# Hybrid attention and mixture block on one core: later input loads, numerators swapped in their own buffer, second weights taken by quarters, and new instruction orders

## The reference, cut to what matters

```python
x = x + attn_a(layernorm(x), w_qkv, w_o)
x = x + ffn(layernorm(x), gate_w, base_w, base_b, lora_A, lora_B)
x = x + attn_b(layernorm(x), wq, wk, wv, wo)
x = x + ffn(layernorm(x), gate_w, base_w, base_b, lora_A, lora_B)

def attn(x, w):
    q, k, v = split(x @ w)
    q, k = rope(q), rope(k)
    p = softmax(causal(q @ k.T * 0.25))
    return (p @ v) @ w_o

def ffn(x):
    w, sel = top_k(x @ gate_w.T, 2)
    w_full = one_hot(sel) * softmax(w)
    lora = (x @ lora_A.T) weighted by w_full, @ lora_B.T
    return x @ base_w.T + base_b + 2.0 * lora
```

## Time and profile before

| | |
|---|---|
| median of 3 runs | 764.03 us (762.78 to 766.94) |
| the profiled execution | 763.37 us, span 761.6 us |
| mean granted TensorE clock | 0.982 |
| TensorE matmul busy | 728.8 us (96%), 4404 instructions |
| VectorE busy | 584.9 us (77%) |
| GpSimd busy | 529.4 us (70%) |
| ScalarE busy | 495.6 us (65%) |
| chain that ended last, PE's share | 82% |

### The profile page before, as it was taken

The page is one execution under the profiler, slowest core; times in us unless marked ns, Lnnn a source line. Parts: engine busy times, 40 slices in busy tenths (PEclk is TensorE's granted clock), DMA queues, the critical chain, the costliest instruction groups (busy, mean ns, idle before and its releaser), DMA issues.

```text
span 761.6 us, 15193 instructions
## 1 busy us (share of the span) xinstructions
PE 728.8 (96%) x4404; PEld 564.2 (74%) x4404; DVE 584.9 (77%) x2756; ACT 495.6 (65%) x1103; POOL 529.4 (70%) x625
## 2 busy tenths in 40 slices
PE   6788999999999999899999999999999999999896
PEld 4685667887777877677787788777787788757575
DVE  4577777887796978679797887879788887769453
ACT  5636567767676767767676876767675776665632
POOL 3266685948587785978778896859788694965522
PEclk8997989999999999999999999999999999999999
DMA  8543534353535447354545635353544535353110
GB/s 308 159 127 66 128 84 119 91 144 105 126 101 151 118 120 186 113 119 108 150 112 161 151 98 139 104 133 100 158 112 123 142 91 116 105 115 90 44 43 28
DMA packets 53356, 91.15 MB, mean 120 GB/s; under 512 B 8916, under 2 KB 21716, under 8 KB 53272
## 3 DMA queue, kind: packets, MB, share of 16 engines
q1 hardware_dynamic: 50968, 89.13, 43.9%
q10 hardware_dynamic: 2304, 1.05, 0.5%
HBM read 24.08 MB, written 10.42 MB: 45 GB/s over the span
## 4 chain that ended last, share of the span: by engine, by line
PE 82%; DMA 4%; DVE 4%; ACT 3%; POOL 3%; SPq 2%; issue 1%; ACTq 0%; POOLq 0%; DVEq 0%
PE SB L447 11%; PE T L463 11%; PE SA L426 7%; PE T L405 5%; PE T L406 5%; PE T L407 5%; PE T L475 4%; PE T L476 4%; PE T L477 4%; PE T L499 4%; PE T L501 4%; PE T L500 4%; PE SA L430 4%; PE T L385 3%; PE T L486 2%; DMA QK<-R 2%
## 5 line engine op out<-in xcount | busy, mean ns | idle before, releaser
L983 DVE CUSTOM_DVE_ANT_0 SA<-SA,mask 128x128 f32<-128x128 f32 (+1 forms) x1024 | 334.1, 386 | 54.7 <-PE SA L426 27.4
L771 ACT ACTIVATE PT<-SB 128x512 f32<-128x512 f32 x384 | 221.0, 599 | 75.6 <-PE SB L447 56.5
L1154 POOL TENSOR_SCALAR_AFFINE_SELECT PT<-PT 128x512 f32<-128x512 f32 x256 | 163.1, 655 | 69.5 <-ACT PT L771 69.3
L447 PE MATMUL SB<-QK 100*128 100x512 f32 x384 | 157.7, 420 | 5.2 <-ACT PT L771 4.3
L983 DVE DVE_READ_ACCUMULATOR2_ANT nm<- 128x1 f32 x1024 | 142.2, 139 | 0.0
L405 PE MATMUL T<-XH,WQh 128*128 128x256 f32 x384 | 111.2, 290 | 3.0 <-DVE XL L949 3.0
L406 PE MATMUL T<-XL,WQh 128*128 128x256 f32 x384 | 109.2, 284 | 0.0
L407 PE MATMUL T<-XH,WQl 128*128 128x256 f32 x384 | 109.1, 284 | 0.0
L426 PE MATMUL SA<-QK 96*128 96x512 f32 x256 | 104.9, 428 | 1.2 <-DVE nm L983 0.9
L447 PEld LDWEIGHTS SB<-QK 100*128 100x128 f32 x384 | 73.2, 194 | 28.9 <-ACT PT L771 8.6
L463 PE MATMUL T<-PT,V 128*32 128x512 f32 x768 | 89.0, 596 | 0.1
(11 more groups left out here) (105 smaller groups left out, 1602.5 us busy)
## 6 DMA issues: line engine op xcount, KB each, us to landing
QK<-Rh SPq DMA_DIRECT2D x64, 256.0 KB, 3.9
QK<-R SPq DMA_DIRECT2D x64, 192.0 KB, 4.1
Qs<-Qf SPq DMA_DIRECT2D x64, 128.0 KB, 2.4
QK<-R SPq DMA_DIRECT2D x64, 128.0 KB, 2.8
ND<-sums SPq DMA_DIRECT2D x62, 128.0 KB, 2.6
ND<-EF SPq DMA_DIRECT2D x33, 128.0 KB, 2.1
mid<-X SPq DMA_DIRECT2D x16, 256.0 KB, 2.0
X<-mid SPq DMA_DIRECT2D x8, 512.0 KB, 3.8
```

Of the source, the lines that this page charges most:

```text
L447: e.matmul(SB[k % 2][:, :].rearrange("p (j q) -> p j q", j=4), keys(p, 100)[:, u % 2, i // 2, :], queries(p, 100)[:, :, min(i, 1), :], sta ...
L771: e.activation(PT[:, k % RING, :], SB[k % 2][:, :], ACT.Exp, scale=0.25).then_inc(S["ex"], 1)
L983: ins = e.tensor_tensor_reduce(x, x, mask[:, 256 - n:256], 1.0, LOWEST, ALU.add, ALU.max, nm[:, p % 2, 0, 8 * a + 2 * h + q:8 * a + 2 * h ...
L1154: e.affine_select(out=blk, in_=blk, compare_op=ALU.is_ge, fill=0.0, base=0, pattern=[[0, 4], [1, 128]], channel_multiplier=-1).then_inc(S[ ...
```

## The change

It moves, in all five lists, most calls to other places, and it edits seven things besides.

```diff
+VLOW = (0, 1, 2, 3, 18, 20)
+PLOW = tuple(k for k in range(25) if k not in VLOW)
...
+        def low_of(k):
+            return ("wlv", VLOW.index(k) + 1) if k in VLOW else ("wlp", PLOW.index(k) + 1)
...
         def normalise(e, w, h):
             w.wait_ge(S["rr"], 32 * (h + 1))
             w.wait_ge(S["xc"], 16 * (h + 1))
+            w.wait_ge(S["ol"], h)
...
-            e.tensor_tensor(n, n, d, ALU.mult).then_inc(S["mu"], 1)
+            e.tensor_tensor(n, m, d, ALU.mult).then_inc(S["mu"], 1)
...
             def xc(h):
...
-                e.dma_start(ND[1:P:2, 0, :, :, :], EF[0:P:2, 1, :, :, :]).then_inc(S["xc"], 16)
...
             def rd(h):
...
+                w.wait_ge(S["lc"], 16 * (h + 1))
+                w.wait_ge(S["xc"], 16 * h)
+                e.dma_start(EF[1:P:2, 0, :, :, :], EF[0:P:2, 1, :, :, :]).then_inc(S["xc"], 16)
...
+            def rows(b):
+                e.dma_start(X[:, 2 * b:2 * b + 2, :],
+                            x_in[256 * b:256 * b + 256, :].rearrange("(t p) d -> p t d", p=P)).then_inc(S[f"x{b}"], 16)
+
+            def added():
+                w.wait_ge(S["kr"], 1)
+                e.dma_start(QK[96:100, 1:4, 1024:1536].bitcast(F32), QK[96:100, 0, 1024:1536].unsqueeze(1).to_broadcast(
+                    [4, 3, 512]).bitcast(F32)).then_inc(S["krd"], 16)
+                e.dma_start(bias[:, :], bias_in).then_inc(S["c_bias"], 16)
+                e.dma_start(iota[:, :], iota_in).then_inc(S["c_iota"], 16)
...
-            for b in range(2, XR):
-                e.dma_start(X[:, 2 * b:2 * b + 2, :],
-                            x_in[256 * b:256 * b + 256, :].rearrange("(t p) d -> p t d", p=P)).then_inc(S[f"x{b}"], 16)
-            e.dma_start(bias[:, :], bias_in).then_inc(S["c_bias"], 16)
-            e.dma_start(iota[:, :], iota_in).then_inc(S["c_iota"], 16)
-            sw(0, 2); sw(0, 0); sw(0, 1); st(0, 1); st(1, 1); st(2, 1); st(3, 1); st(0, 0); st(1, 0); st(0, 2)
...
+            sw(0, 2); rows(2); sw(0, 0); sw(0, 1); rows(3); rows(4); added(); st(0, 1); st(1, 1); st(2, 1)
+            st(3, 1); st(0, 0); st(1, 0); st(0, 2); st(2, 0); st(1, 2); st(2, 2); st(3, 2); st(3, 0); sw(1, 2)
...
+            def idle(n, c=2, t=SB[1]):
+                w.wait_ge(S["c_id"], 16)
+                for i in range(n):
+                    e.matmul(t[:, 0:128 * c], iden[:, :], iden[:, :].unsqueeze(1).to_broadcast([P, c, 128]), start=True,
+                             stop=True, skip_group_check=True)
...
+                elif s == NB - 1:
+                    ins.then_inc(S[f"qw{k}"], 1)
...
+                elif n in (NT - 2, NT - 1):
+                    ins.then_inc(S[f"ow{k}"], 1)
...
-                if 17 <= k < 21:
+                if 17 <= k < 20:
+                    w.wait_ge(S[f"qw{k - 17}"], 3)
+                if k == 20:
                     for b in range(3):
-                        w.wait_ge(S[f"q{b}"], 8)
-                if 21 <= k:
-                    w.wait_ge(S["om"], 16)
+                        w.wait_ge(S[f"q{b}"], NB)
+                if 21 <= k < 24:
+                    w.wait_ge(S[f"ow{k - 21}"], 2)
+                if k == 24:
+                    w.wait_ge(S["om"], NT)
...
             def oe(h, q, t):
-                w.wait_ge(S["ol"], h)
-                w.wait_ge(S["kr"], 4)
+                w.wait_ge(S["mu"], h)
...
-                copy(EF[:, :, q, :, :], src)
+                ins = copy(EF[:, :, q, :, :], src)
                 if h == LAST:
...
-                else:
-                    copy(ND[:, 0, q, :, :], src[:, 0, :, :]).then_inc(S[f"oe{q}"], 1)
+                ins.then_inc(S[f"oe{q}"], 1)
...
             def krows():
                 w.wait_ge(S["c_kr"], 16)
-                for n in range(4):
-                    copy(QK[96:100, n, 1024:1536],
-                         ND[96:100, 0, :, :, :].rearrange("r q j t -> r (q j t)")).then_inc(S["kr"], 1)
+                copy(QK[96:100, 0, 1024:1536],
+                     ND[96:100, 0, :, :, :].rearrange("r q j t -> r (q j t)")).then_inc(S["kr"], 1)
```

More of the change, by code:

```diff
@@ L691, in _ @@
-            warm(2, t=SA[0]); front("f", 31, T[3], ("fx", 29)); fA(30, 0, T[1], ("ox", 30)); fA(30, 1, T[1])
-            fA(30, 2, T[1]); fA(30, 3, T[1]); fB(30, 0, T[0], ("ox", 31)); fB(30, 1, T[0])
-            fA(31, 0, T[2], ("fl", 30)); fA(31, 1, T[2]); fA(31, 2, T[2]); fA(31, 3, T[2]); fB(30, 2, T[0])
-            fB(30, 3, T[0]); fB(31, 0, T[3], ("fl", 31)); fB(31, 1, T[3]); fB(31, 2, T[3]); fB(31, 3, T[3])
-            fW(15, T[1], ("fg", 30)); fC(30, T[0]); fC(31, T[3])
+            warm(5); front("a", 0, T[2], ("", -1)); idle(4); front("a", 1, T[2], ("al", 0)); idle(4)
@@ new lines, in _ @@
+            qkv(0, 2, 0, T[3], ("", -1)); qkv(0, 0, 0, T[0], ("", -1)); qkv(0, 2, 1, T[3])
+            front("a", 2, T[2], ("al", 1)); qkv(0, 2, 2, T[3]); qkv(0, 2, 3, T[3]); qkv(0, 0, 1, T[0])
+            qkv(0, 0, 2, T[0]); qkv(0, 0, 3, T[0]); qkv(0, 1, 0, T[1], ("", -1)); qkv(0, 1, 1, T[1])
+            qkv(0, 1, 2, T[1]); qkv(0, 1, 3, T[1]); idle(4); vT(0, T[2], ("al", 2)); idle(7)
+            front("a", 3, T[2], ("ve", 0)); idle(6); qkv(1, 2, 0, T[3], ("qe2", 0))
+            qkv(1, 0, 0, T[0], ("qe0", 0)); qkv(1, 2, 1, T[3]); A(0, 0); A(0, 1); qkv(1, 2, 2, T[3])
@@ new lines, in _ @@
+            qkv(1, 2, 3, T[3]); A(0, 2); qkv(1, 0, 1, T[0]); A(0, 3); qkv(1, 0, 2, T[0]); A(0, 4)
+            qkv(1, 0, 3, T[0]); A(0, 5); qkv(1, 1, 0, T[1], ("qe1", 0)); A(1, 0); qkv(1, 1, 1, T[1])
+            M2(0, T[2], ("al", 3)); idle(1, 1); A(1, 1); qkv(1, 1, 2, T[1]); idle(1, 1); A(1, 2)
+            qkv(1, 1, 3, T[1]); idle(1, 1); A(1, 3); vT(1, T[2], ("ml", 0)); idle(1, 1); A(1, 4); idle(1, 1)
+            A(1, 5); idle(1, 1); A(2, 0); front("a", 4, T[2], ("ve", 1)); B(0, 0); M2(1, T[0], ("qe0", 1))
@@ new lines, in _ @@
+            front("f", 28, T[2], ("ox", 28)); idle(1, t=SA[0]); oM(31, 0, T[0], ("ox", 29)); oM(31, 1, T[0])
+            fA(28, 0, T[2], ("fl", 28)); fA(28, 1, T[2]); fA(28, 2, T[2]); fA(28, 3, T[2])
+            fB(28, 0, T[1], ("oe0", 31)); fB(28, 1, T[1]); front("f", 29, T[3], ("oe1", 31))
+            oM(30, 0, T[2], ("fg", 28)); oM(30, 1, T[2]); fB(28, 2, T[1]); fB(28, 3, T[1])
+            fA(29, 0, T[3], ("fl", 29)); fA(29, 1, T[3]); fA(29, 2, T[3]); fA(29, 3, T[3]); idle(2, t=SA[0])
+            oM(30, 2, T[2]); oM(30, 3, T[2]); oM(31, 2, T[0]); oM(31, 3, T[0]); fB(29, 0, T[3], ("fg", 29))
@@ L697, in _ @@
+            fB(31, 2, T[0]); fB(31, 3, T[0]); fW(15, T[2], ("fg", 30)); idle(2, t=SA[0]); fC(30, T[1])
+            fC(31, T[0])
         @block.scalar
@@ L870, in _ @@
-            oe(6, 1, T[2]); ex(29, 0); ex(29, 1)
+            norm("a", 0); wh(0); wh(1); high("a", 0, T[2]); norm("a", 1); wh(2); wh(3); krows()
+            high("a", 1, T[2]); wh(4); wh(5); wh(6); wh(7); norm("a", 2); norm("a", 3); qe(0, 2, T[3])
+            qe(0, 0, T[0]); high("a", 2, T[2]); qe(0, 1, T[1]); wh(8); wh(9); rh(0, 2); wh(10); wh(11); wh(12)
+            wh(13); wh(14); wh(15); wh(16); ve(0, T[2]); rh(0, 0); rh(0, 1); high("a", 3, T[2]); norm("a", 4)
+            qe(1, 2, T[3]); qe(1, 0, T[0]); mc(0, T[2]); mr(0); qe(1, 1, T[1]); ve(1, T[2]); high("a", 4, T[2])
@@ L939, in _ @@
+            gw(15); lora_high(15, T[2])
         @block.vector
```

790 lines of the change are left out of this document (387 added, 403 removed).

## The result

| | before | after |
|---|---|---|
| median of 11 runs | 763.41 us (759.72 to 768.51) | 772.2 us (766.5 to 776.69) |
| the profiled execution | 763.37 us, span 761.6 us | 772.8 us, span 770.9 us |
| mean granted TensorE clock | 0.982 | 0.984 |
| TensorE matmul busy | 728.8 us (96%) | 730.7 us (95%) |
| VectorE busy | 584.9 us | 592.0 us |

The ratio is 1.0104, with a 95% interval of 1.0070 to 1.0137. ScalarE lost the 18 us of work that the change takes from it. TensorE has 2 us more of work and the span 9.3 us more, so 7 us are idle time that wasn't there. The 1% is clear of the noise and small: the single executions of either kernel spread over 9 to 10 us.

What follows compares the result with a forecast made beforehand. The prediction took TensorE to bound the loop, with savings only outside undisturbed steps. Its terms, 0 - 4 - 3.6 - 5.2 + 0 = -12.8 us, against the 764.03 us median gave 751.2, stated as 751.0 us, range 743 to 760.

Steps and rivals of the forecast that it cites:

- Start: Before A(0,0): shorter swap and fewer krows copies offset by VectorE's wait for late X; 0, between -3 and +2 us.
- Ramp: Until the loop is full: earlier rope of step 1 saves TensorE's maxima wait and a third of the clock's loss; -4 us.
- the wait at 61.99: In the ramp, TensorE's 2.24 us wait for VectorE's maxima, expected to go; its return would show the forecast wrong.
- Switch: Step where second query weights replace the first: releasing quarters singly and two remainders on VectorE; -3.6 us, between -3.8 and 0.
- Tail: End of the kernel: norms behind exponentials, oM pieces behind PV(30), mixture inside a wait; -5.2 us, between 0 and -8.
- The other two terms: In the tail: three oM pieces moved behind PV(30), -2.1 us, and the mixture of tiles 28 and 29 in a wait, -0.7.
- Loop: Undisturbed steps: bounded by TensorE without waits, so the saved copy and later numerators' DMA change nothing; 0 us.
- The slower rival: Loop stalls as A(4s+4,0) misses the keys' lay-out by 1.5 us in each of 12 steps; 769 us, chance 0.08.
- The clock: Rival: a longer pause before A(0,0) lowers TensorE's clock and cancels the early rope's gain; 755.7 us, chance 0.20.

Runs made afterwards that it cites:

- the last experiment: Changed kernel with statistics and keys' rounding later, a GpSimd wait, two weight loads behind the sums, and late loads back ahead of the first swaps: 757.92 us, 0.9927.

## Why the prediction was wrong, step by step

**Forecast 751.0 us, 743 to 760; measured 772.2.** It gave 0.09 to slower. The sum had -12.8 where +9 was found.

- **Start, 0.** By A(0,0) it was right: 43.41 us (42 to 44 forecast, had 43.07; from the first swap's issue 21.8 and 21.2), with the wait of VectorE for X that was named, 3.04 us. The swap took 2.4 us and the copies were out of the chain, and the wait ate both gains. But I priced the late loads only at where they land. SP's time to issue them, 2.0 us in the chain once the wait for X is gone, was in no term. And the swap's gain isn't shown to come from the late loads: with the loads in front it took 2.85 us in the last experiment.
- **Ramp, -4.** The step that failed. What I traced came half true: A(4,0) starts at 74.36 in place of 77.18, 2.8 us earlier, but the second remainder is at 65.4 and not near 61, the clock in 60 to 80 is 0.74 again, and the wait at 61.99, whose 2.24 us were half of the term, came back as 1.61 and 0.35 us from 62.15 on. That was one of my signs of being wrong. From A(0,0) to PV(0) it took 32.6 us, 29.5 before, of which the work that now stands ahead of PV(0) is under 1 us, an estimate from the matmuls' records. All twelve traces with the new orders have 31.0 to 33.8 there, the old orders with three of the edits 29.6, so this loss belongs to the orders and the edits of the start; no run took it apart. And PV(0) to PV(4) took 87.93 us, 82.64 before: 5.3 us more. The keys' remainder of step 2 met a row of GpSimd's instructions and TensorE waited for 3.82 us, with the clock at 0.74 behind it. I had this mechanism in hand, from the pair in the earlier trace rows, and used it at the wrong place and as a fixed factor of 2.3. The Trainium skill ("SBUF — State Buffer", section "SBUF: two separate sides") has it as a lock for the length of an instruction. The trace agrees that the two keep each other out, but here the wait was 4 to 5 us, over four instructions or more, not one. That an earlier rope on GpSimd makes all of it earlier left out that a tighter row on GpSimd is just what can starve VectorE.
- **Switch, -3.6.** Measured +1.3 in the step itself (48.08 against 46.77). The releases by quarters gave nothing measurable (49.02 in the old order). The remainders on VectorE gave 5 us in the traces, against the 2.4 that I had them lose, since they free a slot of Wst earlier. The two loads ahead of the sums took 2.4 us back; I had read the places of the roundings on ScalarE and none of the loads' on SP. The fourth rounding did lose its wait for its load, as forecast.
- **Tail, -5.2.** One of three terms came out: from PV(27) to the end 109.0 us, 112.4 before, so -3.4, and -4.2 from PV(25). B(125,1) to the last B takes 5.3 us, 8.4 before (forecast 6.0), where no norm stands in front of the exponentials now. The other two terms, 2.8 us, aren't found: from the last B to the end are 38.7 us, 38.5 before. No run took the tail apart. That its end is bound by the latencies of the last tiles, as the wait for xn in the earlier trace rows suggests, isn't shown.
- **Loop, 0.** Right for the undisturbed steps (42.7 to 42.9 us) and wrong for steps 7 to 9, which took 43.9 to 44.4, beyond the 43.5 that I had named as a sign of being wrong. The slower rival had the kind of mistake right (a step that has lost its slack, about 1 us in each) but named A(4s+4,0) and the lay-out of the keys; TensorE waited for V, behind a rounding that had been moved ahead of it. That move stood in the diff of ScalarE's loop and was in no term.
- **The clock.** It fell after the wait before A(0,0) (40 to 60: 0.91, before 1.00), as the rival had it. What keeping it up is worth isn't measured: the idle matmuls overran the pause, the moved work didn't keep the clock up, and in both kernels VectorE's maxima made TensorE wait again for 2.17 and 2.18 us.

## What to carry to other kernels

When lists are reordered, price each moved call on every queue that it passes, SP's issue time included, and look at what now stands directly behind a call that can wait. An instruction of VectorE with two SBUF operands has no fixed price beside GpSimd: it may wait for GpSimd's next pause, in one execution and not in the next, so look for an unbroken row there, and either put the pause in or keep such instructions away. Compare two executions from the last event that the edit can't have touched.
